# A graph network's last layer: the maximum in two parts, eight tiles' values made ahead, two exponentials moved

## What is computed

```python
h = tanh(x @ W + b);  inp = x @ W
e = (h @ a)[:, 0];    valid = sum(h, axis=1) != 0
mask = (adj > 0) & valid[None, :]
scores = where(mask, e[None, :], -1e30)
w = where(mask, exp(scores - max(scores, axis=1)), 0)
out = (w / max(sum(w, axis=1), 1e-30)) @ inp
```

## Time and profile before

| | us |
|---|---|
| median of the runs | 2982.97 |
| profiled execution, device time | 2982.94 |
| its span | 2981.0 |
| TensorE matmuls busy | 2909.5 |
| VectorE busy | 2126.0 |
| ScalarE busy | 1921.8 |
| GpSimd busy | 1189.5 |

### The profile page before, as it was taken

One profiled execution on the slowest core, in us unless ns is written; L12 is line 12 of the kernel. 1 busy time (PEld: TensorE's weight loads), 2 busy tenths in 40 slices (PEclk: granted clock), 3 DMA queues, 4 the chain that ended last, 5 costly groups with the idle time before them and its releaser, 6 DMA issues.

```text
span 2981.0 us, 64441 instructions
## 1 busy us (share of the span) xinstructions
PE 2909.5 (98%) x24310; PEld 2540.4 (85%) x24310; DVE 2126.0 (71%) x3899; ACT 1921.8 (64%) x3408; POOL 1189.5 (40%) x1592
## 2 busy tenths in 40 slices
PE   8899999999989999999999999999999999989999
PEld 6889999999989999999998878887888878755555
DVE  5899888888988888888886566566666666562245
ACT  5779999999988999999986445544455444530000
POOL 2572288632236566563221032333333333544222
PEclk9999999999999999999999999999999999999999
DMA  8565100000100000000010000000000000000001
GB/s 194 111 119 102 43 16 12 15 11 11 62 16 12 14 12 14 12 14 11 11 35 12 4 1 4 4 1 4 1 4 4 1 1 1 3 1 0 0 15 43
DMA packets 36266, 70.85 MB, mean 24 GB/s; under 512 B 8298, under 2 KB 21866, under 8 KB 31978
## 3 DMA queue, kind: packets, MB, share of 16 engines
q0 software_dynamic: 4608, 33.56, 6.0%
q1 hardware_dynamic: 30400, 34.49, 3.8%
q10 hardware_dynamic: 1066, 0.26, 0.0%
HBM read 97.47 MB, written 4.39 MB: 34 GB/s over the span
## 4 chain that ended last, share of the span: by engine, by line
PE 90%; DVE 5%; issue 2%; ACT 1%; DMA 1%; POOL 1%; DVEq 0%; ACTq 0%; POOLq 0%
PE bank L1478 21%; PE bank L1481 21%; PE bank L1538 16%; PE bank L1576 13%; PE bank L1484 11%; PE bank L1405 3%; PE bank L1565 2%; PE bank L1552 1%; DVE rings L1924 1%; PE bank L1420 1%; DVE rings L1927 1%; PE bank L1457 1%; DMA arena<-in_adj_dram 1%; DVE rings L1919 1%; ACT above L1049 1%
## 5 line engine op out<-in xcount | busy, mean ns | idle before, releaser
L1478 PE MATMUL bank<-values,rings 128*128 128x195 bf16 x8192 | 1391.9, 248 | 32.4 <-DVE rings L1927 23.0
L1481 PE MATMUL bank<-values,rings 128*128 128x195 bf16 x8192 | 1391.9, 248 | 0.0
L1049 ACT ACTIVATE above<-srow,kpass 128x512 fp8e4<-128x512 f32 x2032 | 1282.2, 709 | 108.4 <-DVE rings L1927 99.1
L1478 PEld LDWEIGHTS bank<-values,rings 128*128 128x128 fp8e4 x8192 | 802.8, 98 | 46.4 <-issue 41.8
L1481 PEld LDWEIGHTS bank<-values,rings 128*128 128x128 fp8e4 x8192 | 802.9, 98 | 0.4
L1924 DVE TENSOR_TENSOR rings<-rings,above 128x512 uint32<-128x512 uint32 x512 | 388.1, 758 | 166.2 <-PE bank L1481 139.1
L1139 ACT ACTIVATE values<-srow,cmul 128x512 f32<-128x512 f32 x256 | 205.9, 815 | 411.5 <-PE bank L1576 410.3
L1927 DVE TENSOR_TENSOR rings<-rings 128x512 uint32<-128x512 uint32 x512 | 425.6, 831 | 17.3
L1576 PE MATMUL bank<-hv,values 128*128 128x257 f32 x1792 | 420.6, 380 | 0.0
L1576 PEld LDWEIGHTS bank<-hv,values 128*128 128x128 f32 x1792 | 335.0, 190 | 69.9 <-issue 25.2
L1484 PE MATMUL bank<-values,rings 128*128 128x390 bf16 x1920 | 318.9, 329 | 10.3 <-DVE values L1963 10.3
(11 more groups left out here) (239 smaller groups left out, 3459.7 us busy)
## 6 DMA issues: line engine op xcount, KB each, us to landing
arena<-in_adj_dram POOLq DMA_DIRECT2D x32, 1024.0 KB, 9.0
srow<-src_dram SPq DMA_DIRECT2D x69, 256.0 KB, 3.2
x<-in_x_dram SPq DMA_DIRECT2D x4, 1024.0 KB, 7.1
out_dram<-x SPq DMA_DIRECT2D x7, 512.0 KB, 2.9
arena<-in_L_gnn_fe_w_dram SPq DMA_DIRECT2D x2, 512.0 KB, 6.2
arena<-in_L_gnn_W_hz_dram SPq DMA_DIRECT2D x1, 1024.0 KB, 7.2
arena<-in_L_gnn_g_w_dram SPq DMA_DIRECT2D x1, 1024.0 KB, 10.5
weights<-in_L_gnn_W_dram SPq DMA_DIRECT2D x3, 256.0 KB, 3.3
```

The source lines that it names most:

```text
L1049: last = act.activation(above[:, k % 2, q, :], srow[:, par, :], ACT.Relu, scale=BIG, bias=kpass[:, p % 2, k * Q + q:k * Q + q + 1], satura ...
L1478: pe.matmul(acc[:, 0:KW], pos[:, k % 2, q, :].bitcast(FP8)[:, rows], v[:, 0:KW], start=start, stop=final, skip_group_check=True)
L1481: last = pe.matmul(acc[:, KP:KP + KW], neg[:, k % 2, q, :].bitcast(FP8)[:, rows], v[:, KP:KP + KW], start=False, stop=final, skip_group_ch ...
```

## The change

In layers 0 and 1 ScalarE makes the two exponentials after the first of the last quad's four h copies rather than after the fourth.

In layer 3 the first eight tiles get a maximum of their own, and their values are made in the rounds. VectorE reduces the first eight scores (`early_max`, after `tanh_scores(4)`). TensorE turns the column into a row in round 7, VectorE reduces that row to one number (`early_one`, r = 8), TensorE spreads it over the partitions by a product with ones in round 8, and VectorE and ScalarE make factors and values in r = 9 to 13, all casts on VectorE. VectorE also makes the first two units' `edge` there. TensorE's first two units then run from these values into banks 4 to 7, the other six into banks 0 to 3 with the chunks in the order 1, 2, 3, then 0 (for the groups behind). The first two units' sums go to `early_sums` in steps 4 and 5 of the first group; in the second group they are multiplied by exp(early maximum - whole maximum) and added. The whole maximum is made as before, after the last score.

```diff
@@ first_tiles @@
+            if l == 3:
+                u = (u + 1) % FIRST_CHUNKS
@@ ScalarE: copy_quad_h, stats @@
                 for i in range(QT):
+                    if l < 2 and q == QUADS - 1 and i == 1:
+                        exps(l)
                     act.wait_ge(s_hps, q * QT + (l * T + i + 1))
...
+            def exps(l):
+                act.wait_ge(s_shift, l + 1)
+                e = emul[:, :, :, :].rearrange("p k h t -> p k (h t)")
+                act.activation(e[:, 1], e[:, 0], ACT.Exp, scale=SLOPES[l]).then_inc(s_expone, 1)
+                act.activation(e[:, 0], e[:, 0], ACT.Exp).then_inc(s_exps, 1)
...
+                if l < 2:
+                    copy_srcT(l)
+                    return
...
                     act.activation(emul[:, 0, 0, :], emul[:, 0, 0, :], ACT.Exp).then_inc(s_exps, 1)
+                    act.activation(early_scale, early_scale, ACT.Exp).then_inc(E.c_scale, 1)
@@ ScalarE: rounds @@
                     tanh3(r)
+                    if r == 9:
+                        act.wait_ge(E.c_shift, 1)
+                        act.activation(early_exp, early_exp, ACT.Exp).then_inc(E.c_exp, 1)
@@ TensorE: group @@
+                early = 2 if l == 3 and first else 0
                 for k in range(BITS):
-                    if first and k % 2 == 0:
-                        pe.wait_ge(s_vfirst, first_values_before(l) + k + 2)
+                    if k < early:
+                        if k == 0:
+                            pe.wait_ge(E.c_vals, 2)
+                            pe.wait_ge(E.l_h, EG)
+                    elif first and k % 2 == 0:
+                        pe.wait_ge(s_vfirst, first_values_before(l) + k + 2 - early)
...
+                        v = early_values[:, k * Q + q, :] if k < early else values[:, slot, k * Q + q, :]
+                        start, final = (k in (0, early) and q == 0), (k in (early - 1, BITS - 1) and q == Q - 1)
...
+                            acc = bank[GT + it if k < early else GT * par + it]
...
+                        if l == 3 and par == 1:
+                            pe.wait_ge(s_vfirst, first_values_before(3) + 2 * FIRST_CHUNKS)
@@ TensorE: rounds, for r in range(4, EG) @@
                     product3(r)
                     if r + 2 < EG:
                         across3(r + 2)
                     if r == 4:
                         g2_product(EG - 1)
+                    if r == 7:
+                        pe.wait_ge(E.c_pmax, 1)
+                        pe.matmul(top_row, smax[:, 0, 1:2], ident[:, :], start=True, stop=True).then_inc(E.c_across, 1)
+                    if r == 8:
+                        pe.wait_ge(E.c_one, 1)
+                        pe.matmul(top_spread, ones_row3, one_top, start=True, stop=True).then_inc(E.c_spread, 1)
@@ VectorE: order of the first group, layer 3 @@
-            FIRST3 = {0: ((first_rests, 0),),
-                      1: ((first_lasts, 0), (first_products, 1), (first_rests, 1), (first_products, 2), (first_lasts, 1)),
-                      3: ((first_rests, 2), (first_products, 3), (first_lasts, 2)),
-                      5: ((first_rests, 3), (first_lasts, 3))}
+            FIRST3 = {0: ((first_rests, 0), (first_lasts, 0)),
+                      2: ((first_products, 1), (first_rests, 1)),
+                      3: ((first_products, 2), (first_lasts, 1)),
+                      4: ((first_rests, 2),),
+                      5: ((first_products, 3), (first_lasts, 2)),
+                      6: ((first_rests, 3),),
+                      7: ((first_lasts, 3),)}
@@ VectorE: stats, layer 3 @@
-                    shifted.then_inc(s_shift, 1)
+                    dve.tensor_tensor(early_scale, early_top, late_top, ALU.subtract).then_inc(s_shift, 1)
@@ VectorE: group @@
+                        if not first or k >= UNITS_AHEAD:
+                            dve.wait_ge(s_unit, unit - 1 + CREDIT)
+                            dve.tensor_scalar(edge[:, r], words, shift[0], ONE, shift[1], ALU.bitwise_and)\
+                                .then_inc(s_sides, 1)
...
+                            if k in (4, 5):
+                                for it in (2 * k - 8, 2 * k - 7):
+                                    summed = sum_parts(3, 1, 0, it, early_sums)
+                                if k == 5:
+                                    summed.then_inc(s_sums, 1)
...
+                        if k == GT and with_early:
+                            summed.then_inc(E.c_summed, 1)
+                            dve.wait_ge(E.c_summed, 1)
+                            dve.wait_ge(E.c_scale, 1)
+                            dve.scalar_tensor_tensor(out=sums[:, 0], in0=early_sums, scalar=early_scale,
+                                                     in1=sums[:, 0], op0=ALU.mult, op1=ALU.add).then_inc(s_sums, 1)
@@ VectorE: rounds @@
+                def early_max():
+                    dve.wait_ge(E.l_score, CHUNK // ET)
+                    dve.tensor_reduce(smax[:, 0, 1:2], scores3[:, :, 0:CHUNK], AX.X, ALU.max).then_inc(E.c_pmax, 1)
+                def early_one():
+                    dve.memset(ones_row3, 1.0)
+                    dve.wait_ge(E.c_across, 1)
+                    dve.tensor_reduce(one_top, top_row, AX.X, ALU.max).then_inc(E.c_one, 1)
+                def early_shift():
+                    dve.wait_ge(E.c_spread, 1)
+                    dve.tensor_copy(early_top, top_spread).then_inc(E.c_max, 1)
+                    dve.wait_ge(E.c_max, 1)
+                    dve.tensor_scalar(early_exp, scores3[:, :, 0:CHUNK], early_top, None, ALU.subtract)
+                    dve.tensor_scalar(early_valid, kscores[:, 0:1, 0:CHUNK], 0.0, None, ALU.not_equal)\
+                        .then_inc(E.c_shift, 1)
...
+                def early_products():
+                    dve.wait_ge(E.c_mul, 1)
+                    for vtmp, factor, columns, _ in early_tiles():
+                        dve.tensor_copy(vtmp[:, 0, :, D:C], factor)
+                        dve.tensor_tensor(vtmp[:, 0, :, 0:D], columns, factor.to_broadcast([P, CHUNK, D]), ALU.mult)\
+                            .then_inc(E.c_big, 1)
+                def early_cast(i):
+                    for kind, (vtmp, _, _, part) in enumerate(early_tiles()):
+                        dve.wait_ge((E.c_big, E.c_rest)[i], kind + 1)
+                        dve.tensor_copy(part[i], vtmp[:, i]).then_inc(E.c_cast, 1)
...
                 tanh_scores(4)
+                early_max()
                 x_stats(EG - 2)
...
                     tanh_scores(r - 1)
                     if r == 8:
                         x_stats(EG - 1)
+                        early_one()
                     if r == 9:
                         x_norm(EG - 1)
+                        early_shift()
+                    if r == 10:
+                        early_mul()
+                        early_products()
+                    if r == 11:
+                        early_cast(0)
+                        early_edges()
+                    if r == 12:
+                        early_rests()
+                    if r == 13:
+                        early_cast(1)
+                        early_lasts()
```

More of the change, by code:

```diff
@@ L434, in gnn_kernel @@
         E.l_score, E.l_inpool = sem("l3_score_made"), sem("l3_tanh_in_by_pool")
+        E.c_pmax, E.c_max, E.c_shift, E.c_exp, E.c_mul = (sem("l3_first_chunk_" + n) for n in (
+            "partition_max", "max", "shifted", "exp", "factor"))
+        E.c_big, E.c_cast, E.c_rest, E.c_vals = (sem("l3_first_chunk_values_" + n) for n in (
+            "multiplied", "cast", "rest", "made"))
+        E.c_across, E.c_one, E.c_spread = (sem("l3_first_chunk_max_" + n) for n in ("across", "one", "spread"))
+        E.c_summed, E.c_scale = sem("l3_first_group_summed"), sem("l3_first_chunk_scale")
         E.gate_in, E.gate, E.parts, E.fused, E.f_var, E.f_rstd, E.f_norm, E.x = (sem("e_out_" + n) for n in (
@@ L595, in gnn_kernel, with early_tiles @@
         edge_last = arena[:, 0:BITS * Q * WORDS].bitcast(U32).rearrange("p (k q w) -> p k q w", k=BITS, q=Q)
+        early_values = arena[:, 0:CHUNK * KP].bitcast(BF16).rearrange("p (n c) -> p n c", n=CHUNK)
+        early_exp, early_valid, early_factor = (emul[:, 1, i:i + 1, 0:CHUNK] for i in range(3))
+        early_top, late_top, early_scale = smax[:, 1, 1:2], smax[:, 1, 0:1], smax[:, 0, 2:3]
+        top_row, top_spread = bank[7][0:1, 0:P], bank[7][:, P:P + 1]
+        one_top, ones_row3 = smax[0:1, 0, 3:4], srow[0:1, 1, GI - P:GI]
+        early_sums = srow[:, :, :].rearrange("p a i -> p (a i)")[:, 0:GT * 2 * C]\
+            .rearrange("p (t k c) -> p t k c", t=GT, k=2)
+        def early_tiles():
+            out = []
+            for kind, vtmp in enumerate((vtmp_dve, vtmp_pool)):
+                part = [early_values[:, :, kind * KW + i * C:kind * KW + (i + 1) * C] for i in range(PARTS)]
+                out.append((vtmp, early_factor.rearrange("p a n -> p n a"), h[:, 0:CHUNK, kind * D:(kind + 1) * D], part))
```

(29 more changed lines are left out.)

17 lines of the change are left out of this document (5 added, 12 removed).

## The result

**2987.29 us** (median of 20 runs, 2985.28 to 2990.14) against 2983.11 for the kernel before on the same chip (20 runs): ratio 1.0015, 95% interval 1.0009 to 1.0021. That is 4.2 us slower, clear of the noise but under the 0.2% named above, so "same", with 2986.9 forecast. The profiled execution took 2987.05 us, its span is 2985.1, 4.1 more than before.

A forecast was written before the change was run, and what follows sets the result against it. TensorE, busy 98% of the span, was taken as the bound. Layer 3's 10.2 + 0.1 - 5.3 = +5.0 and -1.0 in layers 0 and 1 gave +4.0 on 2982.94: 2986.9 us, 8-in-10 range 2980 to 2991.

The forecast's parts named there:

- hold: `product3(9)` later: Layer 3, round 8: TensorE waits for the early maximum's number, made on VectorE behind `x_stats(EG-1)`; +7.3 us.
- slow clock behind it: Layer 3 rounds: after 8.6 us idle TensorE resumes at 1.2 GHz for about 4 us; +2.0 us, bounds 0 and 2.2.
- rounds, VectorE's tail and GpSimd together: Layer 3, rounds behind the wait: catching up -2.5, VectorE's new work in round 13 +2.4, VectorE blocked by GpSimd +1.0 us.
- reduction later (R): Layer 3: the last-score maximum's reduction comes 10.2 us later, 7.3 + 2.0 - 2.5 + 2.4 + 1.0, at 2637.9.
- reduction to unit 2: Layer 3: from the last-score reduction to unit 2's start, 7.18 us as before plus 0.1 for a subtraction.
- six units: Layer 3, first attention group: units 2 to 7 take 18.0 us rather than 23.3 for eight; -5.3 us.
- the two VectorE terms: Layer 3, last rounds: casts and subtractions ahead of `tanh_in(14)`, +2.4 us, and GpSimd's additions blocking VectorE, +1.0 us.
- VectorE beside GpSimd: Layer 3 rounds: GpSimd's four additions lose VectorE up to 0.9 us each; +1.0 us, bounds 0 and 3.6.
- The cast: Layer 3, early values: an f32 to bf16 cast of 128x520 on VectorE takes 0.62 us, between 0.42 and 0.69.
- VectorE becomes the ring's bound: Rival, rounds 10 to 13: all four GpSimd additions collide and casts take 0.69; 2989.8 us, up to 2992; chance 0.22.
- The hold was not made good: Rival, layer 3 rounds: slack absorbs TensorE's wait, full clock, no longer VectorE tail, free additions; 2980.6 to 2981.5 us; chance 0.13.
- No hold: Rival, round 8: the number is there at 2605, so TensorE does not wait; 2977.7 to 2980.1 us; chance 0.05.

The follow-up runs named there:

- e5: The changed kernel with 34 idle 128x256 matmuls put into TensorE's wait for the spread product in round 8; 2991.81 us.
- e9: The changed kernel with idle matmuls in both new TensorE gaps, 18 in round 8 and 8 ahead of unit 2; 2984.10 us.
- e6: The changed kernel with 20 idle 128x256 matmuls between the early units and unit 2, the wait in round 8 left unfilled; 2991.46 us.
- e3: The kernel before with only the exponentials of layers 0 and 1 moved ahead of the h copies; 2983.68 us, ratio 1.0002.
- e1: The changed kernel with `early_one` moved on VectorE from behind `x_stats(EG-1)` to behind `tanh_scores(5)`; 2982.08 us, ratio 0.9999.
- e4: The kernel before with only the early maximum, row product, `early_one`, spread and one copy added, no early values or units; 2989.21 us, ratio 1.0021.
- e11: e8 with three tiles' additions on GpSimd in place of four, tile 13's going to VectorE; 2980.95 us, ratio 0.9995.
- e12: e11 with 10 idle matmuls in TensorE's gap ahead of unit 2; 2980.40 us, ratio 0.9991.
- e7: e1 with VectorE's early shift moved to r = 7 and ScalarE's early exponential behind `tanh3(8)`; 2983.34 us, ratio 0.9998.
- e8: The changed kernel with every early step moved earlier, `early_one` behind `tanh_in(5)`, most others by one round; 2980.97 us, ratio 0.9994.

## Why the prediction was right, term by term

Seven terms of the sum can be read, in us:

| step | forecast | measured | from |
|---|---|---|---|
| hold: `product3(9)` later | +7.3 | +7.85 | from -5.85 to +2.00 on the ruler |
| slow clock behind it | +2.0 | +2.32 | e5, e9 (1.92 in e6) |
| rounds, VectorE's tail and GpSimd together | +0.9 | +0.72 | 21.76 against 21.04 |
| reduction later (R) | +10.2 | +10.89 | sum of these |
| reduction to unit 2 | 7.28 | 6.28 | 2637.33 to 2643.61 |
| six units | 18.0 | 18.67 | to 2662.28 |
| layers 0 and 1 | -1.0 | -1.04 | e3, and the trace after |

Layer 3 came out at +5.36 for +5.0, the whole at +4.1 for +4.0. The steps that decide, the hold and the clock behind it, were forecast with the right cause and nearly the right size. That the total is off by 0.1 to 0.4 us only is luck: single terms below are off by up to 1.2 us, and they cancel.

**The hold** was named with its place, its reason and its size. It is 0.55 us larger: the memset, the reduction and the spread take 0.87 us from 2612.38, not 0.3, and of that the spread alone takes 0.58 at half clock (0.38 in e1).

**Rounds and tail** agree only as a sum. With the hold alone (e4) `product3(9)` to reduction takes 19.60 us, the slow clock included: if that costs the 2.3 measured above, the rounds catch up by 1.4 + 2.3 = 3.7, not 2.5. The early work on top costs 24.08 - 19.60 = 4.5, not the 3.4 of the two VectorE terms. Both were sized too small, by 1.2 and 1.1 us, with opposite signs.

**VectorE beside GpSimd** shows in the timeline after, GpSimd's additions (L940) and VectorE:

```profile
2622.75 1.56 POOL L940 TENSOR_TENSOR values<-hv,bvec 128x512 f32<-128x512 f32 x1 [0.90 <-ACT hv L1251]
...
2623.28 1.06 DVE L2510 COPY vtmp_pool<-emul 128x8 f32<-128x8 f32 x1
...
2625.55 0.42 DVE L2518 CAST arena<-values 128x520 bf16<-128x520 f32 x1
2625.89 1.49 DVE L2518 CAST arena<-vtmp_pool 128x520 bf16<-128x520 f32 x1
...
2628.66 0.69 DVE L2524 TENSOR_TENSOR values<-values,arena 128x520 f32<-128x520 f32 x1
2629.28 1.58 DVE L2524 TENSOR_TENSOR vtmp_pool<-vtmp_pool,arena 128x520 f32<-128x520 f32 x1
```

Three early instructions take 0.89, 1.07 and 0.89 us longer than their like beside them, 2.85 in all, while an addition of GpSimd runs; a score takes 0.80 for 0.41 beside the fourth. That is 3.2 us. So the rule of the Trainium skill that I weighed, by which each addition blocks in full, was nearer than my 1.0, as the loss of the new instructions goes. But in the kernel before all four additions meet an instruction of VectorE as well: three meet scores (1.30, 1.01 and 1.12 for 0.41, 2.2 us), and the first meets one of `x_norm(EG-1)`, which I had overlooked:

```profile
2615.76 1.34 DVE L2308 TENSOR_SCALAR x<-x,zrow 128x256 f32<-128x256 f32 x1 [0.49 <-POOL zrow L839]
```

It takes 0.41 at 2614.85, so the kernel before loses 3.1 us in all. Against it the collisions cost 0.1 more, not 1.0. Against e4, where the hold had spread the rounds and they cost 1.2 (scores of 0.81, 0.63, 0.81 and 0.63), they cost 2.0 more, a part of the 4.5 above. The term thus had the right mechanism and the wrong count; the rest of the 4.5, some 2.5 us by this count, is VectorE's own new work. It also reckoned with two-input instructions alone. Here a copy and a cast are blocked, and above a `tensor_scalar`; the Trainium skill ("SBUF — State Buffer", "Who interferes with whom") says that copy, cast and `tensor_scalar` can take the shared port pair too, and this trace agrees.

**The cast** takes 0.42 us (2625.55), the lower bound, not 0.62.

**Reduction to unit 2** is the term with a wrong reason: I carried the 7.18 us of the earlier trace rows over whole, and 1.0 us of it was the late start of GpSimd's all-reduce, which is gone when GpSimd has been free for longer.

**Six units** take 0.67 more. I put the clock's worth here at 0.3 to 0.4 because VectorE would bound the group anyway; e9 has at most 0.83, e11 and e12 nothing. That VectorE bounds it is so (5.29 of 5.40 us busy in 2643.60 to 2649.00).

**The rivals.** That VectorE becomes the ring's bound is not what decided the kernel after, where moving the hold alone gives back 5.3 us (e1); but VectorE is busy all of 2623 to 2633 there, so it does pace the last rounds, and in every version without the hold it sets their end (e7, e8, e11). The hold was not made good, and it was there. "No hold" priced the early work at 3.4 us of R; e7 and e8 show 5.0 and 5.1. So what the early units save (30.48 us from reduction to group's end before, 24.1 in the best case) is nearly eaten by the later reduction, even without a hold.

What stays open: how R would come out with the four casts on ScalarE or with GpSimd's additions gone altogether. Neither was tried.

## What to carry to other kernels

In hand-ordered queues compare times, not round numbers: "r = 8" is over at 2604.5 us on TensorE and at 2612.4 on VectorE, and the wait at the head of the leading engine's queue cost it the whole distance, and its clock behind it. When such a wait is gone, look for the next (here ScalarE's), and then add up the engine that the new work was given to: it had 2.3 us free of 15.2, and got 6.3. The slow clock cost 1.9 to 2.3 us in the rounds, where VectorE waited for what TensorE makes, and 0 to 0.8 in a group that VectorE paces.

## What the runs showed of the hardware

- **GpSimd's all-reduce needs a lead.** Where VectorE's reduction came 4.8 to 5.3 us after GpSimd's last instruction had ended, the all-reduce started 6.13 (before), 5.97 (e3) and 6.04 us (e4) after that end; in the eleven other runs GpSimd had been idle for 6.59 us or more, and it started 0.32 to 0.33 us behind the reduction. The Trainium skill ("GPSIMD Engine Reference", "2.1 Instruction dispatch") tells of a code load of about 6 us at the first call of a freshly loaded GpSimd kernel, with no instruction of its own in the profile; these rows agree in size. That it is such a load was not shown here, and this all-reduce is not the first of the program.
- **A collision is charged in full.** A copy of 128x8 that takes 0.17 us took 1.06, a 0.42 us cast 1.49. GpSimd's additions, mostly 1.09 to 1.27 us where they began first, took up to 1.61 (e6) where an instruction of VectorE was already running.
- **A cast costs like the edge instruction.** SBUF to SBUF, f32 to bf16, 128x520: 0.42 us (128x512 uint32 in L2210: 0.43), against 0.69 for the f32 to uint8 cast out of PSUM, 128x512.
- **A 128x256 f32 matmul counts as two** in the trace's numbers (36 for 18) and takes 0.436 us in a row at full clock (34 in 14.84 us, e5).
